# One ScalarE square root for both norms in a fused involution and mixture-of-experts block, the first norm a period sooner, and a different share of the products for GpSimd

## The reference, cut to what matters

```python
x = x + involution(_ln_c(x))      # norm over the 128 channels of a pixel, eps 1e-6
t = _to_tokens(x)                 # 12544 tokens of 128 channels
t = t + moe(_ln_t(t))             # norm over the channels of a token, eps 1e-5; 8 experts, top 2

# both norms:      (v - mean) / sqrt(var + eps)
# involution:      h = x.reduce_w + b;  kern = h.span_w + b        49 taps for each of 16 groups
#                  out = sum over the 49 taps of kern * shifted x
# moe:             softmax of router logits, the best two experts, gates scaled to sum 1
#                  y = w2 . (silu(w1 . x) * (w3 . x)) for each chosen expert, weighted and summed
```

## Time and profile before

| | us |
|---|---|
| median of 3 runs (1501.6 to 1506.93) | 1502.02 |
| the profiled execution | 1498.94 |
| its span | 1497.1 |
| PE busy, of the span | 1243.9 (83%) |
| DVE busy | 1122.8 (75%) |
| POOL busy | 1112.2 (74%) |
| ACT busy | 579.5 (39%) |

### The profile page before, as it was taken

The page is one execution under the profiler, slowest core; times in us unless marked ns, Lnnn a source line. Parts: engine busy times, 40 slices in busy tenths (PEclk is TensorE's granted clock), DMA queues, the critical chain, the costliest instruction groups (busy, mean ns, idle before and its releaser), DMA issues. The chain is left out here.

```text
span 1497.1 us, 23125 instructions
## 1 busy us (share of the span) xinstructions
PE 1243.9 (83%) x7667; PEld 1015.6 (68%) x7667; DVE 1122.8 (75%) x1663; ACT 579.5 (39%) x1960; POOL 1112.2 (74%) x788
## 2 busy tenths in 40 slices
PE   4898878788988989899899898899989887587771
PEld 2676767676766777677787777777778676465661
DVE  5998888988898998888889898888889943222220
ACT  4333333334443444444345343454434244133230
POOL 4787979784686887678788687877778875665665
PEclk9999898998999999999999999999999999899996
DMA  4111111112232242332324232243322445666652
GB/s 124 41 60 48 59 49 59 49 31 88 53 79 60 69 97 63 88 78 60 85 59 103 62 86 62 60 100 83 71 58 48 105 119 129 174 137 134 145 117 25
DMA packets 93346, 120.40 MB, mean 80 GB/s; under 512 B 11531, under 2 KB 72428, under 8 KB 93082
## 3 DMA queue, kind: packets, MB, share of 16 engines
q1 hardware_dynamic: 53802, 90.97, 20.0%
q0 software_dynamic: 39424, 27.96, 13.3%
HBM read 78.92 MB, written 42.65 MB: 81 GB/s over the span
## 5 line engine op out<-in xcount | busy, mean ns | idle before, releaser
L851 DVE TENSOR_TENSOR prod<-kern_ps,xn 128x896 f32<-128x896 f32 x592 | 627.9, 1082 | 65.7 <-PE kern_ps L586 63.2
L586 PE MATMUL kern_ps<-h_stack,span 98*128 98x448 f32 x1372 | 466.3, 426 | 112.7 <-DVE prod L851 72.1
L1088 POOL TENSOR_TENSOR acc_p<-acc_p,prod 128x896 f32<-128x896 f32 x192 | 435.9, 2270 | 74.1 <-DVE prod L851 69.4
L1109 POOL DMA_INDIRECT out<-y_tok,idx x224 | 351.6, 1570 | 137.4 <-issue 66.2
L601 PE MATMUL acc_ps<-ident_sb,prod 128*112 128x128 f32 x2864 | 388.4, 280 | 0.0
L601 PEld LDWEIGHTS acc_ps<-ident_sb,prod 128*112 128x112 f32 x2864 | 341.3, 137 | 37.9 <-DVE x L1053 7.8
L586 PEld LDWEIGHTS kern_ps<-h_stack,span 98*128 98x128 f32 x1372 | 227.1, 200 | 205.5 <-DVE prod L851 121.5
L1097 POOL DMA_INDIRECT xs<-rows_x,slots x224 | 219.0, 978 | 61.0 <-issue 41.3
L536 PEld LDWEIGHTS bank<-w2b,hid 114*128 114x128 f32 x1344 | 181.7, 202 | 50.7 <-DVE xf_lo L1046 26.0
L536 PE MATMUL bank<-w2b,hid 114*128 114x128 f32 x1344 | 190.1, 288 | 26.2 <-DVE xf_lo L1046 15.9
L780 ACT ACTIVATE silu<-h_ps 114x512 f32<-114x512 f32 x132 | 79.0, 598 | 235.0 <-PE h_ps L627 235.0
(11 more groups left out here) (154 smaller groups left out, 1349.9 us busy)
## 6 DMA issues: line engine op xcount, KB each, us to landing
wb<-wexp SPq DMA_DIRECT2D x56, 684.0 KB, 5.4
xb<-xs SPq DMA_DIRECT2D x56, 264.0 KB, 3.0
w2b<-in_w SPq DMA_DIRECT2D x56, 171.0 KB
xt<-in_x SPq DMA_DIRECT2D x28, 224.0 KB, 3.4
out<-x SPq DMA_DIRECT2D x28, 224.0 KB, 2.6
wexp<-wb SPq DMA_DIRECT2D x8, 684.0 KB, 3.2
xs<-rows_x,slots POOLq DMA_INDIRECT x224, 2.3
out<-y_tok,idx POOLq DMA_INDIRECT x224
```

The costliest lines, as they stand in the source:

```text
L586: last = mm(kern_ps[:, g % 2, i, 0:N], span[:, k * C:(k + 1) * C], h_stack[:, t % 2, :], start=True, stop=True)
L851: v.tensor_tensor(pair_rows(dst), kern.rearrange("p i (r w) -> p i r w", w=W), taps, ALU.mult).then_inc(s_prod, 1)
L1088: g_.tensor_tensor(acc_p[:], acc_p[:], prod[:, (t * TAPS + u) % PRING, :], ALU.add).then_inc(s_padd, 1)
L1109: g_.indirect_dma_start(out=out, out_offset=bass.IndirectOffsetOnAxis(ap=idx[:, b % XBRING, q:q + 1], axis=0), in_=y_tok[:, b % 2, q * C:( ...
```

## The change

It has three parts, and what follows from them.

- **One root.** In step 9 ACT takes one Sqrt over the `veps` of both norms (`root`), 112 x 8, the last thing of its step. DVE takes the reciprocal in its step 10 (`reciprocal`), ahead of unit 10, and POOL multiplies by minus the mean in its step 11 (`shifts`). The power on POOL is gone. The two preparing roots stand in steps 4 and 18 of the period ahead of tile 0.
- **The first norm a period sooner.** Statistics of tile t stand in steps 0 to 3 of period t-2, and its normalising in steps 14 and 15 (that of tile 1 moves into the period ahead of tile 0). The second norm's halves move from steps 11 and 12 to 12 and 13, and the transposes of `ln2` on PE from step 14 to 15.
- **Shares.** From tile 8 on POOL takes nine units (0, 2, 4, 6, 9, 12, 15, 18, 21) where it took eight (0, 3, ..., 21), in eight additions for seven. PE takes 12 for 13; DVE's four stay.

The diff, cut to its core:

```diff
-BY_POOL = [tuple(range(0, 21, 2)) if t < LATE else tuple(range(0, 22, 3)) for t in range(TILES)]
+BY_POOL = [tuple(range(0, 21, 2)) if t < LATE else (0, 2, 4, 6, 9, 12, 15, 18, 21) for t in range(TILES)]
-J_X1, J_STAT2, J_RSTD2, J_NORM2, J_XN2, J_LG = 5, 6, 9, 11, 14, 17
-J_STAT1, J_RSTD1, J_NORM1, J_XN, J_H = 0, 4, 6, 9, 21
+J_X1, J_STAT2, J_ROOT, J_NORM2, J_XN2, J_LG = 5, 6, 9, 12, 15, 17
+J_XN, J_H = 9, 21
+
+STAT1_AT = [FIRST, FIRST + 14] + [at(t - 2, 0) for t in range(2, TILES)]
+NORM1_AT = [FIRST + 6, FIRST + 20] + [at(t - 2, J_NORM2 + 2) for t in range(2, TILES)]
+
+ROOTS = [(FIRST + 4, [("ln1", 0)]), (FIRST + 18, [("ln1", 1)])]
+for _p in range(TILES + 1):
+    ROOTS.append((at(_p, J_ROOT), [("ln1", _p + 2)] * (_p + 2 < TILES) + [("ln2", _p - 1)] * (_p > 0)))
...
+            def root(n):
+                for stage, t in ROOTS[n][1]:
+                    act.wait_ge(s_stat[stage], 4 * (t + 1))
+                if n:
+                    act.wait_ge(s_rstd, n)
+                act_f(std[:, sides(n), :], veps[:, sides(n), :], ACT.Sqrt).then_inc(s_std, 1)
...
-                    act.wait_ge(s_rstd[stage], 2 * (t + 1))
+                    act.wait_ge(s_shift, ROOT_OF[(stage, t)] + 1)
...
-                    if j == J_STAT1 + k and p + 1 < TILES:
-                        stat("ln1", p + 1, k)
+                    if S - k in STAT1_AT:
+                        stat("ln1", STAT1_AT.index(S - k), k)
...
-                if J_NORM1 <= j < J_NORM1 + 2 and p + 1 < TILES:
-                    normalise("ln1", p + 1, j - J_NORM1)
+                for n, (at_, _) in enumerate(ROOTS):
+                    if S == at_:
+                        root(n)
...
+                for half in range(2):
+                    if S - half in NORM1_AT:
+                        normalise("ln1", NORM1_AT.index(S - half), half)
...
+            def reciprocal(n):
+                dve.wait_ge(s_std, n + 1)
+                for stage, t in ROOTS[n][1]:
+                    if t:
+                        dve.wait_ge(s_norm[stage], t)
+                v.reciprocal(rstd[:, sides(n), :], std[:, sides(n), :]).then_inc(s_rstd, 1)
...
+                for n, (at_, _) in enumerate(ROOTS):
+                    if S == at_ + 1:
+                        reciprocal(n)
...
-            def rsqrt(stage, t):
...
-                g_.tensor_tensor(rstd[stage][:], veps[stage][:], minus_half[:], ALU.pow).then_inc(s_rstd[stage], 1)
-                pool.wait_ge(s_rstd[stage], 2 * t + 1)
-                g_.tensor_tensor(shift[stage][:], negmean[stage][:], rstd[stage][:], ALU.mult).then_inc(s_rstd[stage], 1)
+            def shifts(n):
+
+                pool.wait_ge(s_rstd, n + 1)
+                g_.tensor_tensor(shift[:, sides(n), :], negmean[:, sides(n), :], rstd[:, sides(n), :], ALU.mult).then_inc(s_shift, 1)
```

More of the change, by code:

```diff
@@ L87, in at @@
     return p * TAPS + j
-J_X1, J_STAT2, J_RSTD2, J_NORM2, J_XN2, J_LG = 5, 6, 9, 11, 14, 17
-J_STAT1, J_RSTD1, J_NORM1, J_XN, J_H = 0, 4, 6, 9, 21
+J_X1, J_STAT2, J_ROOT, J_NORM2, J_XN2, J_LG = 5, 6, 9, 12, 15, 17
[5 more added lines that the diff above has]
+    ROOTS.append((at(_p, J_ROOT), [("ln1", _p + 2)] * (_p + 2 < TILES) + [("ln2", _p - 1)] * (_p > 0)))
+ROOT_OF = {tile: n for n, (_, tiles) in enumerate(ROOTS) for tile in tiles}
 PIECE_J = (3, 4, 5, 7, 8, 10, 12)
@@ L286, in build @@
         square = {k: sb(f"square_{k}", [SUB, SUBS]) for k in ("ln1", "ln2")}
[L287 to L290, removed]
+        veps, std, rstd, negmean, shift = (sb(n, [SUB, 2, SUBS]) for n in ("veps", "std", "rstd", "negmean", "shift"))
         lg = sb("lg", [SUB, GMAX, EXPERTS])
@@ L341, in build @@
         s_stat = {k: sem(f"s_stat_{k}") for k in ("ln1", "ln2")}
-        s_rstd = {k: sem(f"s_rstd_{k}") for k in ("ln1", "ln2")}
+        s_std = sem("s_std")
+        s_rstd = sem("s_rstd")
+        s_shift = sem("s_shift")
         s_norm = {k: sem(f"s_norm_{k}") for k in ("ln1", "ln2")}
@@ L388, in h_at, with side, sides @@
             return kern_ps[0:HC, which, 0, :] if PAIR[m] else (h1_ps, h3_ps)[which][0:HC, :]
+        def side(stage):
+            return ("ln1", "ln2").index(stage)
+        def sides(n):
+            stages = [side(stage) for stage, _ in ROOTS[n][1]]
+            return slice(min(stages), max(stages) + 1)
         def in_psum(g):
@@ L717, in stat @@
                     act.wait_ge(st, n + 3)
-                    act_f(veps[stage][:], square[stage][:], ACT.Identity, scale=1.0 / C, bias=eps[stage][:, 0:1]).then_inc(st, 1)
+                    act_f(veps[:, side(stage), :], square[stage][:], ACT.Identity, scale=1.0 / C, bias=eps[stage][:, 0:1]).then_inc(st, 1)
+            def root(n):
[4 more added lines that the diff above has]
+                act_f(std[:, sides(n), :], veps[:, sides(n), :], ACT.Sqrt).then_inc(s_std, 1)
             def exponentials(g):
@@ L754, in normalise @@
                 for k in (2 * half, 2 * half + 1):
-                    i = act_f(dst[:, k, :], src[:, k, :], ACT.Identity, bias=shift[stage][:, k:k + 1], scale=rstd[stage][:, k:k + 1])
+                    i = act_f(dst[:, k, :], src[:, k, :], ACT.Identity, bias=shift[:, side(stage), k:k + 1],
+                              scale=rstd[:, side(stage), k:k + 1])
                 if half:
@@ L1114, in _ @@
                 p, j = divmod(S, TAPS)
-                if j == J_RSTD1 and p + 1 < TILES:
-                    rsqrt("ln1", p + 1)
-                if j == J_RSTD2 and 0 <= p - 1 < TILES:
-                    rsqrt("ln2", p - 1)
+                for n, (at_, _) in enumerate(ROOTS):
+                    if S == at_ + 2:
+                        shifts(n)
                 if 0 <= p < TILES and j in BY_POOL[p][1:]:
```

11 lines of the change are left out of this document (3 added, 8 removed).

## The result

| | before | changed |
|---|---|---|
| median, us | 1501.81 (4 runs, 1499.71 to 1506.93) | 1537.89 (4 runs, 1535.03 to 1543.54) |
| profiled execution, us | 1498.94 | 1543.54 |
| table loads on ACT | 24 | 71 |

The changed kernel takes 1.0236 times as long (95% interval 1.0213 to 1.0258). 1531 was predicted, in a range of 1500 to 1558.

What follows compares the result with a forecast made beforehand. DVE and PE, each near 90% busy and waiting in turn, were taken to bound the long stretch. Late periods 25.7, early -2, start 5.5, period 0 0.5, tail 0 sum to 29.7 us; predicted 1531, range 1500 to 1558.

Steps and rivals of the forecast that it cites:

- The fork and its price: Step 9 to unit 10: DVE waits for veps, load, Sqrt and reciprocal, 2.1 us late, 0.8 without a load.
- the sign to look for: Trace after: DVE's reciprocal has some 1.7 us of idle time before it in 22 periods, 0.4 in the others.
- What the period gives back: Periods 9 to 27: of each 2.1 us stop, 0.45 and 0.3 come back, leaving 1.35, times 19, 25.7 us.
- The 0.3 for PE's lighter load: Late periods, steps 6 to 9: PE's one sum unit less gives back 0.26 x 1.06 = 0.3 us a period.
- The rival of 1559: ACT's table switch costs twice its load, so 22 stops with a load grow by 28 us; chance 0.07.
- The start: Ahead of tile 0's h_stack: ACT does tile 1's norm first, plus a load, 5.5 us late; bounds 4 and 7.
- The tail: After 1213 us: last shift comes some 0.5 us later and the power goes; 0, bounds -2 and +3.
- The early periods: Periods 1 to 8: stops cost 10.3 us, 12 come back from shorter waits; -2, bounds +10 and -6.
- Period 0: A stop without ln2 in period 0: 0.5 us.
- POOL's ninth unit: Late periods: POOL loses two powers and one shift and gains a 2.375 us addition; nothing over the period.
- the grace of the stop: Late periods: POOL's added addition comes earlier in the tile, but the stop gives POOL 2 us.
- POOL's shift becomes the wait: Rival: POOL reaches step 11 late, ACT normalises late, PE waits in step 15; 1 us a late period, 1550; chance 0.10.

Runs made afterwards that it cites:

- e1_copy: Changed kernel with a Copy, which needs no table, in place of the Sqrt root: 1509.43 us, 1.0038 of the kernel before.
- e8_recip12_old: Changed kernel with reciprocal and shift in step 12 (tail: shift at the root's own step) and POOL's old eight-unit shares: 1510.11 us, 1.0047 of the kernel before.
- e7_oldshares: Changed kernel with POOL's old shares, eight units from tile 8 on: 1537.5 us, 1.022 of the kernel before.
- e4_start: Changed kernel with tile 1's first norm moved behind tile 0's h_stack: 1532.76 us, 1.0183 of the kernel before.
- e4_tail: Changed kernel with only the last norm's shift on POOL moved two steps sooner, to its root's own step: 1529.26 us, 1.0175 of the kernel before.
- e2_shares: Kernel before with only POOL's new shares, nine units from tile 8 on, its norms untouched: 1519.17 us, 1.0108 of the kernel before.
- e3_recip12: Changed kernel with reciprocal two steps and shift one step later, both in step 12, loads kept: 1527.79 us, 1.0173 of the kernel before.
- e11_pow_new: e9_pow with the change's new nine-unit shares for POOL: 1486.43 us, 0.987 of the kernel before.
- e9_pow: Changed kernel with one POOL power for both norms instead of Sqrt and reciprocal, old shares, tile 1's norm as in e4_start: 1486.21 us, 0.9883 of the kernel before.

## Why the prediction was right, and where not

**The fork and its price: right.** DVE's stop at the reciprocal comes where it was put, for the reason given. Predicted 2.1 us late, read 2.04. *e1_copy* takes the load away alone and gets 28.5 us back, *e8_recip12_old* leaves the load and takes the hurry away: periods 9 to 27 come back whole by its profile, about 19 us by medians. The wait before a reciprocal was put at 1.7 us with a load and 0.4 without; it is 2.17 and 0.88. The forecast's own rows give these: DVE was free at 586.00 in the earlier trace rows (0.36 us before unit 10), and with the terms of the price the reciprocal starts at 588.2, 2.2 us later. The price of the stop was right and the sign to look for was worked out wrongly from it. (Periods with both norms are 25, not 27, as the count of reciprocals over 112 x 8 shows.)

**What the period gives back: right in size.** Unit 11's wait for PE went from 0.35 us a late period on the mean (6.6 us over 19) to none; I took 0.45. The 0.3 for PE's lighter load isn't shown: *e7_oldshares* gives PE its unit back and takes as long. What remains of a stop without its load is given back: *e1_copy* has 19 such stops, and its periods 9 to 27 take 859.7 us for 858.9. Net, 25.7 forecast, 23.1 read, and three profiles of the same program differ by 10.

**A switch of tables costs its load and no more.** The Sqrt starts 0.01 us behind its load (601.60 + 1.28, then 602.89), the group of 24 loads has 1.4 us of idle time before it in all, and the loads at the fork cost 28.5/22 = 1.30 us each, give or take 0.2. With this the trace agrees with the load of 1283 ns in the Trainium skill (ScalarE: Activation LUTs, What ACT_TABLE_LOAD costs), and not with its 1380 ns of drain beside it; by that rule 22 loads would cost 58 us, an estimate from the 2.66 us of the Trainium skill, and the measurement decides. The rival of 1559 falls.

**The start: right.** +5.0 for 5.5; `h_stack` at 27.77, forecast 27.9. *e4_start* gets 4.3 us of the start back in its profile (30.4 to 26.1), 5.1 us of the median.

**The tail: the failed step.** "The shift comes some 0.5 later and the power goes. 0; bounds -2 and +3." It cost 8.6 us by *e4_tail*, more than the bound. I priced the instruction and not the place in the queue: the shift went from POOL's step of `veps` to two steps behind it, past two scatters and four output additions of 1.25 and 1.88 us from start to start, 10.0 us (2 x 1.25 + 4 x 1.88). In the late periods of the changed kernel ACT waits for POOL's shift 9.4 us in all; in the tail POOL has no gap, ACT waits 8.54 us for that shift, and the last tiles' routing comes behind it. *e4_tail* shows it alone.

**The early periods: -2 forecast, +1.9 read.** The mechanism is there: PE's waits for the second norm's rows fell to 3.4 us in 2 waits from 11.2 in 7, DVE's for PE to 10.5 from 24.4. But the stop stands in each of these periods (11.7 us in 7 waits). The size is within what one profile can tell: two more profiles of the same program in these periods took 287.2 and 286.4 us, and the mean of the three is 0.2 below the 288.0 of before.

**Period 0: +0.5 forecast, +4.0 read, most of it not by the change.** *e4_tail*, whose program is the same there, has +0.2. The windows (columns of the earlier trace rows) of 46 to 56 and 56 to 66 us, first of the changed kernel, then of *e4_tail*:

```profile
46.00:56.00 10.00, 7.20 (x42) 4.94 (x40) 9.94 (x10) 1.69 (x5) 7.41 (x5) 0.98 0.13 52
...
56.00:66.00 10.00, 9.97 (x47) 8.31 (x48) 7.45 (x8) 3.96 (x19) 5.33 (x3) 0.68 0.05 21
```
```profile
46.00:56.00 10.00, 7.53 (x47) 5.80 (x47) 9.94 (x10) 1.65 (x4) 7.91 (x6) 1.00 0.18 72
...
56.00:66.00 10.00, 9.63 (x63) 7.64 (x62) 9.33 (x11) 3.96 (x19) 4.11 (x2) 1.00 0.00 1
```

From 56 to 66 us the granted clock was 0.68 in the one, a mean between the levels of 1.2 and 2.4 GHz (0.5 and 1), and 1.00 in the other, whose period 0 took 31.1 us. Only 2.4 of the 3.8 us arise there: the unit behind DVE's reciprocal already starts at 45.49 us in the one and at 44.08 in the other, and up to there the granted clock was 1.00 in both. In the 10 us ahead of the fall PE was busy for 7.20 us in the one and 7.53 in the other; what lowers the clock in one execution and not in the other, and what the first 1.4 us are, stays open.

**POOL's ninth unit: the sum was right and half its reason.** I priced it at nothing "over the period", with the grace of the stop. The grace is real: beside the stop it costs nothing (*e7_oldshares*). Without it and with both powers it costs 1.1%, some 16 us (*e2_shares*), and 9 to 16 with POOL free of powers but with the shift at step 12 (*e3_recip12* against *e8_recip12_old*). The rival "POOL's shift becomes the wait" named the mechanism that the waits point to, which this change hides behind its own stop.

One thing stands beside that reading and wasn't separated from it. In each of the four pairs the kernel with the ninth unit, in which PE has one sum unit less a tile, has the lower mean granted clock (medians of the runs): 0.934 and 0.941 (*e2_shares*, before), 0.932 and 0.940 (changed, *e7_oldshares*), 0.932 and 0.939 (*e3_recip12*, *e8_recip12_old*), 0.942 and 0.949 (*e11_pow_new*, *e9_pow*). That can be why a lighter PE never came through as time, or a result of the gaps that it leaves.

**The sum.** By medians the change costs 36.1 us, and 29.7 were forecast. Put by what the experiments undo, the forecast was 28 for the loads (22 x 1.283), 5.5 for the start, 0 for the tail, and about -4 for all the rest, what is left of the stops less all that the periods give back. Measured are 28.5, 5.1, 8.6, and what these leave of 36.1, -6. So the miss is the tail and little else, though a rest found by taking medians of several kernels from each other is good to 5 us or more. How the rest is made up isn't shown; of its parts the 0.3 us a period for PE's lighter load stays without a run that shows it.

## What to carry to other kernels

Joining two small operations is paid by the more urgent of the two: look for who stands still behind the join, not for the busy share of the engine that does it, and give the result a step or two of slack (in *e8_recip12_old* it hides, by medians, some 19 of the 28 us that the loads at the 22 forks cost, by its profile all). A moved instruction comes later by what now stands ahead of it in its queue, and a place that is nearly free in the steady part may be the critical one in the tail. When two edits hide each other, undo each by itself on both kernels: the ninth unit cost some 16 us on the one and nothing on the other.

## What the runs showed of the hardware

- The power on POOL isn't priced by elements alone: 1728 ns over 112 x 8 (*e9_pow*) against 1196 over 112 x 4. Nor by its shape alone: the same instruction has a mean of 1895 ns in *e11_pow_new* and, over 112 x 4, of 1313 in *e2_shares*, the two kernels with the ninth unit beside a power.
- ACT loads a table before it waits for what the activation reads: the 31 loads for Silu had 0.6 us of idle time before them in all, while Silu itself waited 235.7 us over its 132 instances (its group in the page of the changed kernel, below; that of the loads stands further up). In period 13 the load starts at 555.77 us and its Silu at 559.20, after 2.14 us of waiting for PE. Where ACT would have waited longer than a load anyway, the load costs nothing.
- The granted clock over a stretch of 10 us in which two kernels have the same program was 0.68 in one execution and 1.00 in another (56 to 66 us of the changed kernel and of *e4_tail*), and DVE came out of it 2.4 us later.

```profile
L802 ACT ACTIVATE silu<-h_ps 114x512 f32<-114x512 f32 x132 | 79.0, 598 | 235.7 <-PE h_ps L641 197.5
```
